# A graph network kernel on one core: the node update's second product one unit later in the turn

## The chip, the core and the metric

The kernel runs on one core of a Trainium2 chip. The metric is the time of one execution on the device in microseconds (us); smaller is better. The engines named below are TensorE (PE, with its weight loads as PEld), VectorE (DVE), ScalarE (ACT), GpSimd (POOL) and the queue of SyncE (SPq).

## What is computed

The input is a graph with 3,125 nodes of 256 features and 50,000 edges (sorted by target) with 16 features each. Two blocks follow each other, both of the form `x = x + block(relu(layernorm(x)))`. The first is a message network; the second is three graph convolutions over the same edges. Cut to what matters here:

```
h = relu(layernorm(x))
m = relu(concat(h[dst_side], h[src_side], e) @ mW1 + mb1)      # one row for each edge
agg = segment_sum(m @ mW2 + mb2)                                # one row for each node
u = relu(concat(h, agg) @ uW1 + ub1)                            # the node update's first product
x = x + h + (u @ uW2 + ub2)                                     # its second product, and the addition
h = relu(layernorm(x))
x = x + three graph convolutions(h, edges)
```

## The kernel before

Nodes are handled in 25 windows of 128 (`NW = 25`). Four stages run one after the other: `sort_and_embed` ranks the edges and makes the first layer's parts, `edge_mlp` runs the edge network and leaves for each window the sum of its hidden rows, `build_and_update` is the fused stage which the change touches, and `graph_layers` runs the three convolutions.

The fused stage does two things at once.

**Counting the adjacency matrix.** It is made in 175 blocks ("buckets") of 128 x 458 counts, by 568 build steps (`NS`). A step needs two one-hot matrices: `src_oh` (128 x 128, written by POOL on L1230 for three steps of four and by DVE on L1273 for the fourth) and `dst_oh` (128 x 458, always by DVE, L1275). PE multiplies them into one of four PSUM banks of `pC` (L1401). The slots for one-hots are eight deep. ACT reads a finished bank (L1485), prepares it for a later bucket (L1488) and stores the rows to `C_rows` (L1489). SPq lets PE into a bank only when ACT has prepared it (the semaphore `allowed`, L1348).

**The node update of each window.** PE turns the window's sums (`pS`, L1444), DVE copies them to `sT` (L1289); PE makes the message product into `pG` (L1411), DVE adds the bias to make `agg` (L1302); PE turns that (L1454), DVE copies it to `aggT` (L1308); PE makes the first update product into `pU` (`hidden`, L1423), DVE adds the known part (L1315) and takes the maximum with zero (L1317), which is `uT`; PE makes the second update product into `pX` (`update`, L1434, two halves of four matmul instructions in the trace), DVE adds it to the residual (L1295) and takes its statistics (L1297). Many of these tiles lie in one buffer, so the trace calls `sT`, `uT`, `agg`, `aggT` and the weights `sums`.

**The order is written by hand.** There are 27 turns of 9 units (0 to 8). Window i's messages are made in turn i, its first update product in turn i+1, its second in turn i+2. The 568 steps are spread evenly: `first_step(i, u)` is `(9 i + u) * 568 // 243`, so each unit holds two or three steps. PE issues in each unit first the unit's own piece of the update and then the unit's steps. DVE goes through the same units, but in each it first writes one-hots up to five steps beyond the unit's first step (`AHEAD = 5`), and then does the unit's own piece:

```
upto = min(NS, first_step(i, u) + AHEAD)
for s in range(made, upto):
    one_hots(s)
```

So the steps of PE's unit 0 are covered by the one-hots which DVE writes in units 7 and 8 of the turn before, and those of PE's unit 1 reach into the one-hots which DVE writes in its unit 0. DVE's pieces are: unit 0 `sT`, unit 2 the addition, unit 4 `agg`, unit 7 `aggT`, unit 8 `uT` (add and maximum). The copy `aggT` in unit 7 waits until PE has finished the first update product of its unit 8, since that product reads the old `aggT`. Each engine works through its instructions in this order.

Of the kernel before, what the change touches and what calls it, by code (L numbers as in the profile page):

```python
# [21 lines left out]
NW = -(-N // P)  # L22
# [1087 lines left out]
def build_and_update(nc, io, dr, keep):  # L1110


    with ExitStack() as stack:
# [82 lines left out]
        def first_step(i, u):  # L1196

            return min(NS, (i * UNITS + u) * NS // (TURNS * UNITS))

        def known_u(w):  # L1200

            if w < 12:
                return low[:, 2 * w:2 * w + 2, 0:D]
            if w < 14:
                return low[:, 2 * w - 12:2 * w - 10, D:2 * D]
            if w < 17:
                return low[:, 2 * w - 10:2 * w - 8, D:2 * D]
            return late_u[:, w - 17, :, :]
# [25 lines left out]
        def _(dve):  # L1234
# [34 lines left out]
            def one_hots(s):  # L1269
                if s >= SLOTS:  # L1270
                    dve.wait_ge(step_done, s - SLOTS + 2)
                if s % SHARE == 0:
                    v.tensor_scalar(src_oh[:, s % SLOTS, :], keep.iota16[:, :], src_s[:, s:s + 1], None,  # L1273
                                    ALU.is_equal).then_inc(src_own, 1)
                v.tensor_scalar(dst_oh[:, s % SLOTS, :], iota_cw[:, :], dst_s[:, s:s + 1], None, ALU.is_equal  # L1275
                                ).then_inc(dst_ready, 1)

            made = 0
            for i in range(TURNS):
                for u in range(UNITS):  # L1280
# [3 lines that stand above are left out]
                    made = max(made, upto)  # L1284
                    if u == 0 and i < NW:
                        dve.wait_ge(st_done, i + 1)
                        if i >= 1:
                            dve.wait_ge(agg_done, i)
                        v.tensor_copy(sT[:, :], pS[:, :]).then_inc(st_ready, 1)  # L1289
                    if u == 2 and 0 <= i - 2 < NW:  # L1290
                        w = i - 2
                        dve.wait_ge(x_done, w + 1)
                        dve.wait_ge(ub_added, w + 1)
                        r = keep.resid[:, w, :]
                        v.tensor_tensor(r, r, pX[:, 0:D], ALU.add).then_inc(x_ready, 1)  # L1295
                        dve.wait_ge(x_ready, w + 1)
                        v.bn_stats(stats[:, w, :], r).then_inc(stat_ready, 1)  # L1297
                    if u == 4 and i < NW:
                        dve.wait_ge(agg_done, i + 1)
                        if i >= 1:  # L1300
                            dve.wait_ge(at_done, i)
                        v.scalar_tensor_tensor(out=agg[:, :], in0=mb2[:, :], scalar=keep.deg_src[:, i:i + 1],  # L1302
                                               in1=pG[:, 0:D], op0=ALU.mult, op1=ALU.add).then_inc(agg_ready, 1)
                    if u == 7 and i < NW:
                        dve.wait_ge(at_done, i + 1)
                        if i >= 1:
                            dve.wait_ge(u_done, i)
                        v.tensor_copy(aggT[:, :], pG[:, D:2 * D]).then_inc(at_ready, 1)  # L1308
                    if u == 8 and 0 <= i - 1 < NW:
                        w = i - 1  # L1310
                        dve.wait_ge(u_done, w + 1)
                        if w >= 1:
                            dve.wait_ge(x_done, w)
                        dve.wait_ge(h_in[0 if w < HG else 1], 16 * (HG if w < HG else NW - HG))
                        link(v.tensor_tensor(uT.rearrange("p (b n) -> p b n", b=2),  # L1315
                                             pU[:, :].rearrange("p (b n) -> p b n", b=2), known_u(w), ALU.add))
                        v.tensor_scalar(uT, uT, 0.0, None, ALU.max).then_inc(u_ready, 1)  # L1317
# [33 lines left out]
        def _(pe):  # L1351
# [37 lines left out]
            def build_step(s):  # L1389
                if s % GRP == 0:  # L1390
                    _, got = nc.values_load_multi_w_load_instructions(
                        keep.step_bank[0:1, s:s + GRP], engines=[pe.engine], min_val=0, max_val=(BANKS - 1) * HID,
                        skip_runtime_bounds_check_because="the low bits of a bucket's number, times a bank's size")
                    at.update(enumerate(got))
                pe.wait_ge(allowed, s + 1)
                if s % SHARE:
                    pe.wait_ge(src_ready, s - s // SHARE)
                else:
                    pe.wait_ge(src_own, s // SHARE + 1)
                pe.wait_ge(dst_ready, s + 1)  # L1400
                mm(pC[:, bass.ds(at[s % GRP], CW)], src_oh[:, s % SLOTS, :], dst_oh[:, s % SLOTS, :], start=False,  # L1401
                   stop=False, skip_group_check=True).then_inc(step_done, 1)

            def message(i, half):
                if half == 0:
                    pe.wait_ge(st_ready, i + 1)
                    if i >= 1:
                        pe.wait_ge(agg_ready, i)
                        pe.wait_ge(at_ready, i)
                for k in range(2 * half, 2 * half + 2):  # L1410
                    last = mm(pG[:, 0:D], sT[:, k * P:(k + 1) * P], mw2[:, k, :], start=(k == 0), stop=(k == 3))  # L1411
                if half == 1:
                    last.then_inc(agg_done, 1)

            def hidden(w, m):
                if m == 0:
                    pe.wait_ge(at_ready, w + 1)
                    if w == 0:
                        pe.wait_ge(deg_copied, KP)
                    else:  # L1420
                        pe.wait_ge(u_ready, w)
                for k in range(2):
                    last = mm(pU[:, m * P:(m + 1) * P], uw1[:, 2 * (m // 2) + k, (m % 2) * P:(m % 2 + 1) * P],  # L1423
                              aggT[:, k * P:(k + 1) * P], start=(k == 0), stop=(k == 1))
                if m == 3:
                    last.then_inc(u_done, 1)

            def update(w, half):
                if half == 0:
                    pe.wait_ge(u_ready, w + 1)  # L1430
                    if w >= 1:
                        pe.wait_ge(x_ready, w)
                for k in range(2 * half, 2 * half + 2):
                    last = mm(pX[:, 0:D], uT[:, k * P:(k + 1) * P], uw2[:, k, :], start=(k == 0), stop=(k == 3))  # L1434
                if half == 1:
                    last.then_inc(x_done, 1)

            for i in range(TURNS):
                for u in range(UNITS):
                    if u == 0 and i < NW:  # L1440
                        if i >= 1:
                            pe.wait_ge(st_ready, i)
                        for k in range(4):
                            last = nc.tensor.transpose(pS[:, k * P:(k + 1) * P],  # L1444
                                                       keep.sums[:, 2 * i * HID + k * P:2 * i * HID + (k + 1) * P], keep.ident[:, :])
                        last.then_inc(st_done, 1)
                    if 1 <= u <= 2 and 0 <= i - 2 < NW:
                        update(i - 2, u - 1)
                    if 3 <= u <= 4 and i < NW:
                        message(i, u - 3)  # L1450
                    if u == 7 and i < NW:
                        pe.wait_ge(agg_ready, i + 1)
                        for k in range(2):
                            last = nc.tensor.transpose(pG[:, D + k * P:D + (k + 1) * P], agg[:, k * P:(k + 1) * P],  # L1454
                                                       keep.ident[:, :])
                        last.then_inc(at_done, 1)
                    if 5 <= u <= 8 and 0 <= i - 1 < NW:
                        hidden(i - 1, u - 5)
                    for s in range(first_step(i, u), first_step(i, u + 1)):
                        build_step(s)  # L1460
# [554 lines left out]
```

## Time and profile before

| what | value |
|---|---|
| time of the runs | 2148.41 us median of 3 (2143.78 to 2148.63) |
| time of the profiled execution | 2150.04 us |
| its span, first to last instruction | 2148.2 us |
| mean granted TensorE clock | 0.914 of full speed |
| busy share PE, DVE, POOL, ACT | 86%, 72%, 58%, 37% |
| the fused stage's build steps | 1274 to 1592 us of the span |

Busy shares are those of the whole span; the stages differ in what limits them, so the fused stage has to be read by itself. A wait in square brackets in the rows below is the idle time of an engine before an instruction, with the instruction that ended it. A row of several instructions gives the start of the first and the time from there to the end of the last. A wait of an engine that is not the bound costs nothing.

### The profile page before, as it was taken

Reading aid. Unit: us, or ns where it says so; the run is one execution under the profiler, and the core shown is the slowest. Engines: PE = TensorE matmul, PEld = TensorE weight load, DVE = VectorE, ACT = ScalarE, POOL = GpSimd, SP = SyncE. Lnnn points to the kernel's source line nnn. Section 1 sums busy time; section 2 is a strip of 40 time slices with the busy share of each in tenths; the row PEclk is TensorE's granted clock in tenths of the full one; section 3 lists DMA queues with packets and bytes.
Section 4 is the critical chain, followed back from the end, with each engine's and each line's share of the span. In section 5 each row is a group of like instructions: output and inputs, shape, how many; then the busy total and the mean of one; then the engine's idle time right before and its main releaser. Section 6 shows DMA issues by size and latency. Waiting matters only on the chain. (4 is left out here: it accounts for less than half of the span.)

```text
span 2148.2 us, 34105 instructions
## 1 busy us (share of the span) xinstructions
PE 1856.5 (86%) x8860; PEld 1252.2 (58%) x8860; DVE 1543.6 (72%) x4318; ACT 795.9 (37%) x1973; POOL 1241.1 (58%) x1461
## 2 busy tenths in 40 slices
PE   3677877775399999999999969998969999999997
PEld 2344454443155555555555536666647788788776
DVE  8877777776299988999988968988877345335332
ACT  0221222221155555555555536655662122113000
POOL 3777777777687777777777739998967000000000
PEclk7676777787699999999999979999999999999999
DMA  5111111111376666666666862212244234343232
GB/s 157 43 55 51 56 56 56 56 56 51 92 199 190 190 191 185 189 190 191 189 188 189 176 187 69 67 63 65 70 119 148 80 114 121 96 120 118 89 118 89
DMA packets 181702, 254.09 MB, mean 118 GB/s; under 512 B 29245, under 2 KB 144762, under 8 KB 181515
## 3 DMA queue, kind: packets, MB, share of 16 engines
q0 software_dynamic: 47888, 126.25, 21.6%
q1 hardware_dynamic: 101186, 99.11, 15.0%
q10 hardware_dynamic: 32440, 26.55, 3.8%
q8 instruction: 79, 1.29, 0.3%
q14 instruction: 109, 0.88, 0.1%
HBM read 202.35 MB, written 49.37 MB: 117 GB/s over the span
## 5 line engine op out<-in xcount | busy, mean ns | idle before, releaser
L971 POOL DMA_INDIRECT brow<-B_rows,rows x440 | 464.8, 1056 | 178.5 <-DVE pre L1074 109.8
L372 POOL DMA_INDIRECT src_list<-ring,ring_row x392 | 400.0, 1021 | 151.5 <-issue 117.6
L1865 PE MATMUL pO<-F,y 128*128 128x512 f32 x1728 | 436.4, 406 | 9.8 <-DVE y L1685 6.6
L1865 PEld LDWEIGHTS pO<-F,y 128*128 128x128 f32 x1728 | 326.8, 190 | 89.0 <-DVE y L1685 6.8
L1002 PE MATMUL pEdge<-A,turned 128*128 x880 | 333.2, 490 | 0.0
L1074 DVE TENSOR_TENSOR pre<-pEdge,brow 128x1024 f32<-128x1024 f32 x220 | 268.7, 1221 | 50.9 <-PE pEdge L1002 42.6
L1230 POOL TENSOR_SCALAR src_oh<-iota,src_s 128x128 bf16<-128x128 bf16 x426 | 281.1, 676 | 31.2 <-PE pC L1401 30.0
L1011 PE MATMUL pNode<-hid_whole,oh 128*128 128x512 f32 x440 | 227.7, 599 | 20.9 <-DVE sums L1092 20.9
L1681 DVE CAST F<-raw 128x512 fp32r<-128x512 uint16 x432 | 173.8, 439 | 66.8 <-PE pO L1865 61.6
L1036 ACT ACTIVATE turned<-pTurn 128x256 fp32r<-128x256 bf16 x220 | 84.8, 386 | 313.3 <-PE pTurn L990 313.3
L1275 DVE TENSOR_SCALAR dst_oh<-iota_cw,dst_s 128x458 bf16<-128x458 f16 x568 | 187.0, 376 | 0.0
L1401 PE MATMUL pC<-dst_oh,src_oh 128*128 128x458 bf16 x568 | 160.2, 365 | 29.7 <-SPq L1348 22.1
L1092 DVE SCALAR_TENSOR_TENSOR sums<-sums,going_on,pNode 128x512 f32 x220 | 163.2, 742 | 24.8 <-issue 23.7
L1002 PEld LDWEIGHTS pEdge<-A,turned 128*128 128x128 f32 x880 | 171.3, 195 | 11.8
L1013 PE MATMUL pNode<-hid_upper,oh 128*128 128x512 f32 x220 | 174.5, 793 | 0.0
L1000 PE MATMUL pEdge<-we_rows,turned_e 96*128 96x512 bf16 x440 | 170.3, 387 | 1.3 <-DVE pre L1074 0.9
L814 PE MATMUL pP<-U,upto 128*128 128x182 bf16 x385 | 48.3, 275 | 134.0 <-DVE posf L577 134.0
L1082 DVE SCALAR_TENSOR_TENSOR hid_lower<-pre,hid_upper 128x512 fp32r<-128x512 f32 x220 | 150.0, 682 | 0.0
L1485 ACT CAST c_rows<-pC 128x458 uint16<-128x458 f32 x175 | 94.7, 541 | 133.5 <-PE pC L1401 111.8
L1044 ACT ACTIVATE hid_whole<-pre 128x512 f32<-128x512 f32 x220 | 139.9, 636 | 6.4 <-DVE pre L1074 6.4
L1048 ACT ACTIVATE hid_upper<-pre 128x512 fp32r<-128x512 f32 x220 | 136.6, 621 | 0.0
L814 PEld LDWEIGHTS pP<-U,upto 128*128 128x128 bf16 x385 | 36.0, 110 | 144.0 <-DVE posf L577 132.2
(290 smaller groups left out, 3038.9 us busy)
## 6 DMA issues: line engine op xcount, KB each, us to landing
raw<-C_rows SPq DMA_DIRECT2D x72, 768.0 KB, 4.4
C_rows<-c_rows ACTq DMA_DIRECT2D x175, 114.5 KB, 1.7
rows<-src_list SPq DMA_DIRECT2D x110, 100.0 KB, 2.6
brow<-B_rows,rows POOLq DMA_INDIRECT x440, 3.7
U_parts<-part_u SPq DMA_DIRECT2D x25, 256.0 KB, 2.1
B_rows<-bst SPq DMA_DIRECT2D x25, 256.0 KB, 2.1
src_list<-ring,ring_row POOLq DMA_INDIRECT x392
sums<-U_parts SPq DMA_DIRECT2D x17, 256.0 KB, 5.8
```

The costliest lines, as they stand in the source:

```text
L372: nc.gpsimd.indirect_dma_start(dr.src_list[:, :, :].rearrange("p t w -> (p t) w"), bass.IndirectOffsetOnAxis(ap=ring_row[:, k % RING, t:t ...
L971: nc.gpsimd.indirect_dma_start(brow[:, t % BR, :], None, dr.B, bass.IndirectOffsetOnAxis(ap=rows_i[:, m % LCS, j, 1:2], axis=0)).then_inc( ...
L1000: mm(to, turned_e[:, p % 2, n * P:(n + 1) * P], keep.we[:, :], start=True, stop=False)
L1002: last = mm(to, turned[:, p % 2, n * P:(n + 1) * P], keep.A[:, 2 * HID + k * HID:][:, bass.ds(at[p], HID)], start=False, stop=(k == 1))
L1011: mm(pN[p % 2][:, :], oh[:, q % OHQ, j, :].bitcast(F32), whole[:, p % WHOLE, :], start=True, stop=False)
L1013: mm(pN[p % 2][:, :], oh[:, q % OHQ, j + 1, :], upper[:, p % SPLIT, :], start=False, stop=False)
L1074: v.tensor_tensor(pre[:, p % 2, :], pE[p % 2][:, :], brow[:, at_row:at_row + 2, :].rearrange("p t n -> p (t n)"), ALU.add).then_inc(pre_re ...
L1092: v.scalar_tensor_tensor(out=keep.sums[:, bass.ds(at[p], HID)], in0=keep.sums[:, bass.ds(at[max(p - 1, 0)], HID)], scalar=keep.going_on[:, ...
L1230: nc.gpsimd.tensor_scalar(src_oh[:, s % SLOTS, :], keep.iota16[:, :], src_s[:, s:s + 1], None, ALU.is_equal).then_inc(src_ready, 1)
L1275: v.tensor_scalar(dst_oh[:, s % SLOTS, :], iota_cw[:, :], dst_s[:, s:s + 1], None, ALU.is_equal).then_inc(dst_ready, 1)
L1681: v.tensor_copy(F[:, n % FS, :], raw[:, m % RAWS, n % RAWW, :]).then_inc(f_ready, 1)
L1865: last = mm(pO[m % 2][half][:, :], y[:, win, part, half * P:(half + 1) * P], F[:, n % FS, :], start=(win == 0 and part == 0), stop=False)
```

## The change

The second update product of window i-2 moves from PE's units 1 and 2 to its units 2 and 3 of turn i. The addition of its result, with the statistics, moves from DVE's unit 2 to its unit 4, where it stands ahead of `agg`. PE's unit 3 then holds the second half of the product and the first half of the message product; unit 1 holds nothing but its steps. No instruction is added or removed, and no transfer moves.

```
                        v.tensor_copy(sT[:, :], pS[:, :]).then_inc(st_ready, 1)
-                    if u == 2 and 0 <= i - 2 < NW:
+                    if u == 4 and 0 <= i - 2 < NW:
                         w = i - 2
                         dve.wait_ge(x_done, w + 1)
...
                         last.then_inc(st_done, 1)
-                    if 1 <= u <= 2 and 0 <= i - 2 < NW:
-                        update(i - 2, u - 1)
+                    if 2 <= u <= 3 and 0 <= i - 2 < NW:
+                        update(i - 2, u - 2)
                     if 3 <= u <= 4 and i < NW:
                         message(i, u - 3)
```

## Rows read from the trace of the kernel before

**Rows 1.** The page's head and its first part: busy time of each engine.

```profile
span 2148.2 us, 34105 instructions
PE 1856.5 (86%) x8860; PEld 1252.2 (58%) x8860; DVE 1543.6 (72%) x4318; ACT 795.9 (37%) x1973; POOL 1241.1 (58%) x1461
```

**Rows 2.** The chain that ended last, its first pieces after the fused stage.

```profile
1595.54 6.51 DMA raw<-C_rows
```

**Rows 3.** Busy time by stretch: the stage, turns 11 and 12, two clock stretches.

```profile
core 0: us, PE busy (x) PEld busy (x) DVE busy (x) ACT busy (x) POOL busy (x), PEclk, DMA share, GB/s
1298.00:1592.00 294.00, 263.73 (x1428) 186.50 (x1427) 263.25 (x850) 175.61 (x324) 273.71 (x413) 0.99 0.21 67
1400.62:1412.47 11.85, 10.57 (x60) 7.77 (x59) 10.26 (x33) 6.96 (x13) 11.45 (x17) 1.00 0.19 63
1412.47:1426.31 13.84, 12.26 (x61) 8.62 (x58) 11.30 (x34) 7.17 (x14) 11.50 (x18) 0.88 0.16 53
1412.31:1415.72 3.41, 1.83 (x11) 0.91 (x9) 3.11 (x8) 1.89 (x4) 3.41 (x6) 1.00 0.22 71
1415.72:1419.13 3.41, 3.41 (x9) 2.27 (x10) 2.61 (x10) 1.09 (x2) 2.13 (x4) 0.50 0.00 0
```

**Rows 4.** Waits from 1298 to 1592 us: total, times, longest.

```profile
ACT c_rows L1485 <- PE pC L1401: 93.3, 125, 3.5
DVE sums L1308 <- PE pU L1423: 21.2, 23, 2.1
POOL src_oh L1230 <- PE pC L1401: 18.1, 34, 2.4
PE pX L1434 <- DVE sums L1317: 13.6, 23, 1.0
PE pC L1401 <- SPq L1348: 9.7, 14, 1.5
PE pC L1401 <- DVE dst_oh L1275: 5.3, 15, 0.7
```

**Rows 5.** Waits of PE in the stage's last stretch, 1560 to 1592 us.

```profile
PE pC L1401 <- SPq L1348: 5.6, 6, 1.5
```

**Rows 6.** PE and DVE in order of time, start of turn 11.

```profile
1401.07 0.33 DVE L1275 TENSOR_SCALAR dst_oh<-iota_cw,dst_s 128x458 bf16<-128x458 f16 x1
1401.64 0.36 PE L1401 MATMUL pC<-dst_oh,src_oh 128*128 128x458 bf16 x1 [0.19 <-DVE dst_oh L1275]
1402.51 0.36 PE L1401 MATMUL pC<-dst_oh,src_oh 128*128 128x458 bf16 x1 [0.51 <-DVE dst_oh L1275]
1402.97 0.43 DVE L1317 TENSOR_SCALAR sums<-sums 128x512 f32<-128x512 f32 x1
1403.31 0.72 DVE L1275 TENSOR_SCALAR dst_oh<-iota_cw,dst_s 128x458 bf16<-128x458 f16 x2
1403.45 1.13 PE L1434 MATMUL pX<-sums 128*128 128x256 f32 x4 [0.58 <-DVE sums L1317]
1404.42 0.75 PE L1401 MATMUL pC<-dst_oh,src_oh 128*128 128x458 bf16 x3
```

**Rows 7.** The same at the start of turn 4.

```profile
1322.16 0.72 DVE L1275 TENSOR_SCALAR dst_oh<-iota_cw,dst_s 128x458 bf16<-128x458 f16 x2
1322.30 1.13 PE L1434 MATMUL pX<-sums 128*128 128x256 f32 x4 [0.51 <-DVE sums L1317]
1323.27 0.55 PE L1401 MATMUL pC<-dst_oh,src_oh 128*128 128x458 bf16 x2
```

**Rows 8.** The same at the start of turn 21.

```profile
1524.52 1.13 PE L1434 MATMUL pX<-sums 128*128 128x256 f32 x4 [0.51 <-DVE sums L1317]
1524.66 0.75 DVE L1275 TENSOR_SCALAR dst_oh<-iota_cw,dst_s 128x458 bf16<-128x458 f16 x2
1525.48 0.55 PE L1401 MATMUL pC<-dst_oh,src_oh 128*128 128x458 bf16 x2
```

**Rows 9.** The moved instructions on DVE, turn 11, in order of time.

```profile
1406.35 0.40 DVE L1295 TENSOR_TENSOR resid<-resid,pX 128x256 f32<-128x256 f32 x1
1406.78 0.43 DVE L1297 BATCH_NORM_STATS2 stats<-resid 128x6 f32<-128x256 f32 x1
```

More of the change, by code:

```diff
@@ L1289, in _ @@
                         v.tensor_copy(sT[:, :], pS[:, :]).then_inc(st_ready, 1)
-                    if u == 2 and 0 <= i - 2 < NW:
+                    if u == 4 and 0 <= i - 2 < NW:
                         w = i - 2
@@ L1446, in _ @@
                         last.then_inc(st_done, 1)
-                    if 1 <= u <= 2 and 0 <= i - 2 < NW:
-                        update(i - 2, u - 1)
+                    if 2 <= u <= 3 and 0 <= i - 2 < NW:
+                        update(i - 2, u - 2)
                     if 3 <= u <= 4 and i < NW:
```

## Prediction

> **What bounds the kernel now.** I read the page's busy times first [rows 1]. They say little of this change, since every engine's share is an average over four stages. The chain that ended last begins only at 1595 us, with the load of the counts that the fused stage stored [rows 2]. The last stage therefore starts when the fused stage ends, and whatever the fused stage gains or loses reaches the end in full. So the whole question lies between 1274 and 1592 us.
>
> There the busy times by stretch come next [rows 3]: from 1298 to 1592 us PE is busy for 263.7 of 294 us, DVE for 263.3, POOL for 273.7. Three engines have nearly the same load, so busy time does not name the bound and the waits must [rows 4]. ACT waits for PE for 93 us, DVE for 21 us (the copy `aggT`), POOL for 18 us. PE waits for others for less than 30 us: 13.6 us for `uT`, 5.3 us for `dst_oh`, 9.7 us for a bank. The loop that sets the pace is one between PE and DVE. At the end of a turn PE finishes the first update product, which frees DVE's `aggT` copy; DVE then writes one-hots, makes `uT`, and writes more one-hots, while PE runs out of work; from there on PE is dense until the next end of a turn. The order of time at the start of turn 11 shows it [rows 6]: PE stands for 0.19, 0.51 and 0.58 us, and for nothing in the rest of that row of work.
>
> **The change, part by part.** Nothing is added, so the cost is one of order.
>
> *What is taken away.* PE no longer stands before `update` for `uT`: by the time it comes to unit 2, `uT` is long done. That is up to 13.6 us over 23 waits [rows 4], a mean of 0.59 us.
>
> *What comes in its place.* Unit 1 now holds only its steps. By the kernel's order DVE's unit 8 has written one-hots for 2.67 steps past the start of the turn, and unit 0's PE steps use 2.33 of them. The steps of unit 1, which reach to 4.67, need those of DVE's unit 0, and DVE writes these after `uT`. Before, PE covered that time with half an update product, which needed only `uT`. Now it has nothing to cover it with, and waits for the last `dst_oh` of unit 1, which is later than `uT`.
>
> For turn 11 [rows 6]: a one-hot that ended at 1401.07 + 0.33 = 1401.40 let its step start at 1401.64, so the way from DVE to PE is 0.24 us. Two steps in a row take 0.55 where one takes 0.36 [rows 7], so each further step is 0.19 to 0.20 us. The last one-hot that unit 1 needs ends at 1403.31 + 0.72 = 1404.03. Its step starts at 1404.27, and the update product at 1404.47, where it started at 1403.45: 1.02 us later. The three steps that used to follow it are by then done, and are worth 3 x 0.195 = 0.59 us. Net: PE stands 0.43 us later in its work than before.
>
> For turn 4 [rows 7]: last one-hot 1322.16 + 0.72 = 1322.88, product at 1323.32 in place of 1322.30, less two steps (0.39): 0.63 us. For turn 21 [rows 8]: last one-hot 1524.66 + 0.75 = 1525.41, product at 1525.85 in place of 1524.52, less 0.39: 0.94 us. Nine turns have three steps in unit 1 as turn 11 has, the rest two. The mean of the three is 0.67 us. PE is dense from there to the end of the turn, DVE's `aggT` copy waits for PE and so comes later by the same amount, and the next turn begins that much later. Nothing in the loop gives it back. Over the 24 turns from 2 to 25: 24 x 0.67 = 16 us. By the lowest and the highest of the three it is 10 and 23 us.
>
> *The addition on DVE.* L1295 and L1297 take 0.40 and 0.43 us [rows 9], some 0.86 us with the gap between them, and move from unit 2 to unit 4. Behind them on DVE now stands `agg` and then the one-hots of unit 5. PE needs `agg` only in unit 7. The one-hots of units 3 and 4 come 0.86 us sooner, but PE did not stand for them. What could be gained is DVE's wait for `pX`, and what could be lost is an `agg` that is late; with three units of some 1.2 us between, I take nothing for both. At the most the addition lies bare in each turn, 24 x 0.86 = 21 us, or gives as much, but DVE's 21 us of waits for PE [rows 4] speak against both.
>
> *What swallows part of it.* Where a bank is late, PE waits for ACT through SPq, and a PE that comes later waits less. There are 9.7 us of such waits [rows 4], 5.6 us of them from 1560 us on [rows 5], where the last turns follow ACT. I take the last two turns' delay as hidden there (0.94 + 0.67 = 1.6 us) and 1 us elsewhere. The bound from below is 0, from above 9.7 us.
>
> *The clock.* In turn 12 PE stood still for 1.58 us of the 3.41 us before 1415.72 and then ran at a granted clock of 0.50 (1.2 GHz) until 1419.13; the turn took 13.84 us in place of turn 11's 11.85 [rows 3]. A fall costs 2.0 us. My gaps at the start of turn 11 come to 0.19 + 0.51 us as now, and then, in place of 0.58 us, one of about 0.9 before the second step of unit 1, so about 1.6 us in place of 1.3. More gaps can only make falls likelier, though the clock stayed at 1.00 through turn 11. I take half a fall more than now, 1 us; the bounds are one fewer (-2 us) and five more (+10 us).
>
> The Trainium skill's page "TensorE: Matmul & The Clock Gate" (section "A second HAM failure mode: psum-queue depth-cycling") says that short idles between groups of matmuls can be enough to make the clock go to and fro. This trace agrees in one turn: 0.50 after gaps none of which was long. By that rule alone each turn might fall, and the sum would be some 48 us more; the same gaps of 1.3 us in turn 11 left the clock at 1.00 [rows 3], so the sum above doesn't follow it.
>
> *Sum.* 16.1 - 1.6 - 1.0 + 1.0 = 14.5 us. The profiled execution took 2150.04 us, of which 1.84 lie outside its span of 2148.2 and stay. It gives 2164.5. That execution was 1.6 us above the median of the runs shown, 2148.41, from which I would get 2162.9. I forecast 2164 us.
>
> **The rivals.** A measurement of this kernel can tell about 0.3%, 6.4 us, from no change.
>
> *The clock falls in many turns.* For it: PE stands longer at the start of each turn, and turn 12 fell after standing for 1.58 us [rows 3]. Against: the gaps grow by a third only, and those of turn 11 left the clock alone. Five falls more are 14.5 + 9 = 24 us, a fall in each of ten turns 35 us: 2173 to 2184 us.
>
> *The wait is absorbed, and no change shows.* The banks are the mechanism: if PE's later arrival saves all of its 9.7 us of waits for SPq, and the least of the three turns holds (10 us), nothing is left; with one clock fall fewer the time is 2148 to 2154. Against it: ACT waits 93 us for PE, so in most of the stage it is ACT that is early.
>
> *Faster: the wait for `uT` goes and nothing replaces it.* This would be so if the one-hots for unit 1 were ready when PE comes to it, that is, if the last of them ended before 1402.5 in turn 11 rather than at 1404.03. It decides at that point: each turn then wins its 0.59 us. With 13.6 us of waits gone, and perhaps the two falls of the clock (4 us), it gives 2136 down to 2132 us. For it: the wait on `uT` is real and the longest item of PE's list, and DVE has 0.86 us less to do before its unit 3. Against it: that work stands behind the one-hots in question, not ahead of them, and `uT` itself is ahead of them.
>
> **How the numbers follow.** My forecast (a later one-hot takes the wait's place, few falls more) has 0.66, its own range 2157 to 2171. More falls of the clock have 0.14, all slower. Absorbed has 0.11, mostly within 0.3%. Faster has 0.09, of which 0.07 goes beyond 0.3%. The forecast's lower end lends 0.03 to no change. Slower: 0.80, same: 0.13, faster: 0.07. The range is 2152 to 2174: it leaves out the faster case and the upper part of the falls.
>
> **What would show it.** Right: in the stage PE's wait for L1317 is gone, and its wait for `dst_oh` (L1275) grows from 5.3 to some 30 us; the start of turn 4 shows one gap of about 1 us inside unit 1's steps; turns are 12.3 us in place of 11.8; DVE's wait before L1308 grows from 21 to some 35 us; POOL and ACT wait more; the last stage has the same length. The addition's own wait (L1295) is near nothing. Wrong: turns no longer than before, which means that one-hots were ready or that another engine had been the pace; new waits of PE before L1454, which means that `agg` is late; or a granted clock in the stage well under 0.99, which is the rival with the falls.

## The result and the profile after

The changed kernel took 2166.07 us (median of 5 runs, 2164.43 to 2169.25), the kernel before 2147.29 us in the same comparison. The ratio is 1.0089 with a 95% interval of 1.0076 to 1.0103: slower by 19 us, with 16 to 22 us inside the interval. The forecast was 2164 us, slower, from a loss of 14.5 us.

The head of the page answers to [rows 1]: the work is the same, the span is 15 us longer.

```profile
span 2163.2 us, 34105 instructions
PE 1858.8 (86%) x8860; PEld 1252.1 (58%) x8860; DVE 1540.1 (71%) x4318; ACT 795.2 (37%) x1973; POOL 1237.0 (57%) x1461
```

The start of turn 4 after the change, PE, DVE and POOL in order of time; it answers to [rows 7]:

```profile
1323.60 5.66 POOL L1230 TENSOR_SCALAR src_oh<-iota,src_s 128x128 bf16<-128x128 bf16 x9
1325.33 0.42 DVE L1308 COPY sums<-pG 128x256 f32<-128x256 f32 x1 [0.62 <-PE pU L1423]
1326.42 0.72 PE L1401 MATMUL pC<-dst_oh,src_oh 128*128 128x458 bf16 x2 [0.17 <-SPq L1348]
1327.16 0.43 DVE L1317 TENSOR_SCALAR sums<-sums 128x512 f32<-128x512 f32 x1
1327.51 0.72 DVE L1275 TENSOR_SCALAR dst_oh<-iota_cw,dst_s 128x458 bf16<-128x458 f16 x2
1328.19 0.64 PE L1401 MATMUL pC<-dst_oh,src_oh 128*128 128x458 bf16 x2 [1.06 <-POOL src_oh L1230]
1328.67 1.03 PE L1434 MATMUL pX<-sums 128*128 128x256 f32 x4
```

PE has finished unit 0's two steps at 1327.14 and stands for 1.06 us until the first step of unit 1. The row names POOL as what ended the wait. It was not: POOL wrote nine one-hots in a row without idle, and the one of this step had ended 2.8 us earlier. DVE's two one-hots start at 1327.51, behind the maximum of `uT`, and their rows end at 1327.95 and 1328.23; PE's steps start 0.24 us behind each, at 1328.19 and 1328.47. The product follows at 1328.67. From the end of the first update product (0.10 us ahead of `aggT`, so 1325.23) it starts 3.44 us on. In the kernel before that product of turn 3 ended at 1319.82, and the second one started 1322.30 - 1319.82 = 2.48 us on [rows 7]. The gap has moved from ahead of the product (0.51 us) to ahead of the steps (1.06 us).

The waits, in the same order as [rows 4] but from 1298 to 1608 us, the longer stage:

```profile
POOL src_oh L1230 <- PE pC L1401: 33.2, 52, 1.8
DVE sums L1308 <- PE pU L1423: 23.7, 24, 1.5
PE pC L1401 <- DVE dst_oh L1275: 19.7, 31, 1.6
DVE sums L1302 <- PE pG L1411: 14.4, 21, 1.2
PE pC L1401 <- SPq L1348: 12.7, 19, 2.0
PE pC L1401 <- POOL src_oh L1230: 8.0, 13, 1.1
DVE resid L1295 <- PE pX L1434: 0.9, 1, 0.9
```

PE's wait for L1317 (13.6 us) is gone from the list. Its waits on L1401 put down to DVE and POOL were 5.3 us and almost nothing; they are now 19.7 + 8.0 us. The names are not to be trusted here, for SPq no more than for POOL: in turn 7 a wait of 0.97 us is put down to SPq, and it too ended 0.24 us behind the step's `dst_oh`. The distance to the step's own `dst_oh` is the better sign. In turns 2 to 25 the changed kernel's steps have 58 waits of at least 0.15 us, and 43 of them end 0.24 us behind the end of that one-hot. Waits with this sign (0.24 us, in a few cases up to 0.30) come to 5.8 us in the kernel before and to 27.4 us in the changed one. Of these, 22.4 us stand before steps of unit 1, where the kernel before has none.

**Where the 15 us between the two profiled spans lie.** I cut both traces at the first build step, at the end of the first update product in turn 1 and in turn 25 (24 turns, 2 to 25, lie between), and at the first matmul of the last stage. The rows give busy time by stretch, for the 24 turns of the kernel before and then for the piece behind them up to the last stage:

```profile
core 0: us, PE busy (x) PEld busy (x) DVE busy (x) ACT busy (x) POOL busy (x), PEclk, DMA share, GB/s
1296.68:1578.76 282.08, 257.20 (x1403) 183.57 (x1401) 254.18 (x800) 170.46 (x314) 265.61 (x401) 0.99 0.21 67
1578.76:1595.82 17.06, 7.85 (x32) 3.66 (x33) 11.02 (x58) 6.73 (x13) 9.42 (x15) 1.00 0.19 62
```

and for the changed one:

```profile
1300.24:1592.71 292.47, 255.81 (x1404) 181.91 (x1401) 253.49 (x800) 169.74 (x313) 262.92 (x400) 1.00 0.20 65
1592.71:1611.91 19.20, 10.44 (x33) 4.90 (x33) 11.35 (x59) 7.35 (x15) 10.22 (x16) 0.77 0.17 56
```

| piece | before | after | difference |
|---|---|---|---|
| up to the first build step | 1274.4 | 1278.7 | +4.3 |
| from there to the end of turn 1 | 22.3 | 21.5 | -0.8 |
| 24 turns | 282.1 | 292.5 | +10.4 |
| turn 26 and the rest of the stage | 17.1 | 19.2 | +2.1 |
| last stage | 552.4 | 551.3 | -1.1 |

The first piece runs the same instructions in both and is not the change's. The 24 turns of the kernel before hold two falls of the clock, turns of 13.84 and 13.99 us; the other 22 have a mean of 11.56 us. The changed kernel has no fall in these turns, and their mean is 12.19 us. So a turn at full clock has grown by 0.63 us, 24 x 0.63 = 15.1 us, and with the 2.1 us of the end this is 17 us of the 19 measured.

### The profile page after: what moved, and what is told of

Read it like the earlier page. It is cut to its first block and busy times, and to the rows that moved or that the text cites. A ratio compares the mean times of both kernels' runs of the same rounds, so it can differ in the third digit from the quotient of the medians.

```text
span 2163.2 us, 34105 instructions
## 1 busy us (share of the span) xinstructions
PE 1858.8 (86%) x8860; PEld 1252.1 (58%) x8860; DVE 1540.1 (71%) x4318; ACT 795.2 (37%) x1973; POOL 1237.0 (57%) x1461
## 5 line engine op out<-in xcount | busy, mean ns | idle before, releaser
L1401 PE MATMUL pC<-dst_oh,src_oh 128*128 128x458 bf16 x568 | 164.4, 365 | 55.3 <-SPq L1348 25.6
L1401 PEld LDWEIGHTS pC<-dst_oh,src_oh 128*128 128x128 bf16 x568 | 55.9, 98 | 116.7 <-issue 99.0
## 6 DMA issues: line engine op xcount, KB each, us to landing
U_parts<-part_u SPq DMA_DIRECT2D x25, 256.0 KB, 2.1
B_rows<-bst SPq DMA_DIRECT2D x25, 256.0 KB, 2.1
sums<-U_parts SPq DMA_DIRECT2D x17, 256.0 KB, 5.6
```

## The experiments

Each was timed in five rounds against the kernel before. The first four (the addition alone, the product alone, and AHEAD = 7 on both kernels) ran on a chip on which the kernel before takes 2284.63 us (the later ones: 2144.60 and 2146.03), so ratios are compared and not times. The 137 us more lie ahead of the 24 turns, which begin there at 1434 us of the span and not at 1297, so the same loss makes a slightly smaller ratio there: 19 us are 0.88% of 2147 and 0.83% of 2285 us. The length of a turn can be compared directly: it is the mean over those of the 24 turns in which the granted clock stayed at 1.00. That length and the number of falls come from one profiled execution of each kernel.

| kernel | ratio, 95% interval | turn at full clock, us | turns with a fall |
|---|---|---|---|
| before | 1 | 11.56 | 2 |
| the change | 1.0089 (1.0076 to 1.0103) | 12.19 | 0 |
| addition alone | 0.9988 (0.9977 to 1.0000) | 11.62 | 0 |
| product, addition one unit | 1.0090 (1.0073 to 1.0107) | 12.28 | 4 |
| product in units 3 and 4 | 1.0241 (1.0222 to 1.0261) | 13.24 | 11 |
| before, AHEAD = 7 | 0.9990 (0.9979 to 1.0001) | 11.45 | 1 |
| change, AHEAD = 6 | 1.0042 (1.0027 to 1.0056) | 11.85 | 0 |
| change, AHEAD = 7 | 0.9982 (0.9971 to 0.9992) | 11.30 | 0 |
| change, uT behind unit 0's one-hots | 1.0067 (1.0050 to 1.0083) | 12.09 | 1 |
| before, uT first | 1.0043 (1.0027 to 1.0059) | 11.83 | 1 |
| before, uT first, AHEAD = 7 | 0.9955 (0.9939 to 0.9971) | 11.25 | 0 |
| change, uT first, AHEAD = 7 | 0.9996 (0.9987 to 1.0006) | 11.45 | 1 |
| uT first, AHEAD = 7, one in three | 0.9946 (0.9933 to 0.9960) | 11.05 | 0 |
| uT first, AHEAD = 7, one in five | 0.9984 (0.9975 to 0.9993) | 11.46 | 0 |

### Which half of the change costs: the addition alone

Edits to the kernel before:

```
-                    if u == 2 and 0 <= i - 2 < NW:
+                    if u == 4 and 0 <= i - 2 < NW:
```

> The kernel before, with only the addition (L1295) and its statistics moved from DVE's unit 2 to its unit 4; the product stays in PE's units 1 and 2. Theory A (what costs is that PE has nothing to do in unit 1 until DVE's one-hots behind uT are written): no change, 2147 us, within 4 us of the kernel before. Theory B (what costs is the addition standing ahead of agg on DVE, 0.86 us in each turn): most of the 19 us, 2160 to 2166 us, and DVE's waits before agg (L1302) as long as after the change.

Measured: ratio 0.9988, turns of 11.62 us. The addition's place costs nothing. DVE's waits before `agg` did not grow: in the 24 turns they are 0.7 us, where the kernel before has 1.6.

### The product alone

Edits to the kernel before:

```
-                    if u == 2 and 0 <= i - 2 < NW:
+                    if u == 3 and 0 <= i - 2 < NW:
...
-                    if 1 <= u <= 2 and 0 <= i - 2 < NW:
-                        update(i - 2, u - 1)
+                    if 2 <= u <= 3 and 0 <= i - 2 < NW:
+                        update(i - 2, u - 2)
```

> The kernel before, with the product moved to PE's units 2 and 3 and the addition moved by one unit only, to DVE's unit 3, the first at which it can follow the product. Theory A: the loss of the whole change, 2162 to 2168 us. Theory B: within 4 us of the kernel before. If it is slower than the change itself, the addition's later place had bought something, since in unit 3 DVE would stand for the product.

Measured: 1.0090, the whole loss. The waits of its 24 turns show the one difference from the change: DVE stands for the product in unit 3.

```profile
PE pC L1401 <- DVE dst_oh L1275: 19.2, 31, 1.5
DVE sums L1302 <- PE pG L1411: 11.8, 20, 0.7
DVE resid L1295 <- PE pX L1434: 8.6, 9, 2.0
```

Those 8.6 us make the turns 0.09 us longer at most (12.28 against 12.19), and the ratios are the same. The later place of the addition bought DVE free time, and no time of the kernel that these runs can tell.

### The one-hots for unit 1 written ahead of uT

On the changed kernel:

```
-        AHEAD = 5
+        AHEAD = 7
```

> The change, with AHEAD = 7 in place of 5: DVE's unit 8 then writes all one-hots that PE's unit 1 needs, and writes them ahead of uT. The number of one-hots in each unit stays as it was. Theory A: PE's gap of about 1.05 us in unit 1 goes, PE comes to the product about 2.1 us after the end of the first product, when uT is 0.1 to 0.4 us from ready; each turn loses 0.6 to 1.0 us of idle against the change: 2140 to 2150 us, at or under the kernel before. Rival (PE stands in unit 1 for POOL or for a bank, as the trace names them for some of these waits): no change, 2166 us. Rival B: no change either.

Measured: 0.9982, turns of 11.30 us in place of 12.19. The loss is gone, and more. The waits in its 24 turns:

```profile
PE pC L1401 <- SPq L1348: 9.7, 12, 2.2
PE pX L1434 <- DVE sums L1317: 7.4, 16, 0.9
PE pC L1401 <- DVE dst_oh L1275: 1.8, 5, 0.5
PE pC L1401 <- POOL src_oh L1230: 0.6, 2, 0.4
```

In the 24 turns the wait for DVE's one-hots fell from 19.4 to 1.8 us, and with it the one that the trace had put down to POOL, from 7.6 to 0.6 us, although POOL's work and order had not changed. That settles whose wait it was: by the sign of 0.24 us the waits behind a step's own `dst_oh` are 27.4 us under the change and 1.3 us here. What is left is a wait of 7.4 us for `uT`, shorter than the 13.6 us of the kernel before. In whole time 0.9982 of 2147 is 2143 us, inside the 2140 to 2150 that I had given.

### The same on the kernel before

```
-        AHEAD = 5
+        AHEAD = 7
```

> The kernel before, with AHEAD = 7. Theory A: PE's gap at the start of a turn ends with uT, wherever the one-hots are, so that earlier one-hots only lengthen the wait for uT by what they save on dst_oh: within 4 us of the kernel before. Rival (each wait counts by itself): PE's 5.3 us of waits for dst_oh go, 2141 to 2143 us.

Measured: 0.9990, or 2 us less, within the 4 us. The interval (0.9979 to 1.0001) reaches to 4.5 us and so just touches the rival's 4 to 6 us; the time alone doesn't decide between the two, the waits do. Waits in its 24 turns:

```profile
PE pX L1434 <- DVE sums L1317: 25.8, 23, 2.0
PE pC L1401 <- DVE dst_oh L1275: 0.2, 1, 0.2
```

The wait for `dst_oh` went from 5.3 to 0.2 us, and that for `uT` rose from 13.6 to 25.8 us. With the product in unit 1 the gap ends with `uT`, and what PE gets ahead of that is worth little (0.11 us a turn). The sum of the two rose by 7 us although the time did not. I read that as a matter of the record: a step that waits shows its whole 0.36 us as busy, one that follows another adds 0.19 us [rows 6], so a gap broken up by steps counts as less idle than the same gap in one piece.

### Half of the cover

On the changed kernel:

```
-        AHEAD = 5
+        AHEAD = 6
```

> The change with AHEAD = 6. Theory A: one one-hot fewer of those which unit 1 needs stands behind uT, so the last of them comes 0.3 us sooner in each of 24 turns: 7 to 8 us of the loss come back, turns of 11.85 to 11.95 us in place of 12.19, 1.004 to 1.006 of the kernel before. Rival (only a full cover helps, or the loss has another source): 1.009.

Measured: 1.0042, turns of 11.85 us: 0.34 us less than under the change, the length of about one one-hot. The three settings 5, 6 and 7 give 12.19, 11.85 and 11.30 us, so each one-hot that stands ahead of `uT` in place of behind it is paid back by about its own length or more.

### One unit further

Edits to the kernel before:

```
-                    if u == 2 and 0 <= i - 2 < NW:
+                    if u == 5 and 0 <= i - 2 < NW:
...
-                    if 1 <= u <= 2 and 0 <= i - 2 < NW:
-                        update(i - 2, u - 1)
+                    if 3 <= u <= 4 and 0 <= i - 2 < NW:
+                        update(i - 2, u - 3)
```

> One unit further still: the product in PE's units 3 and 4, the addition in DVE's unit 5. Theory A: units 1 and 2 now both follow DVE's one-hots, and the half product that the change still had in unit 2 (some 0.9 us) no longer covers those behind sT. Each of 24 turns loses 0.86 to 0.97 us more than under the change: 21 to 23 us more, 1.018 to 1.020 of the kernel before. Rival (a fixed price for taking the product out of unit 1, whatever comes after): 1.009, as the change.

Measured: 1.0241, more than expected. PE at the start of a turn:

```profile
1337.03 0.60 PE L1444 MATMUL pS<-ident,sums 128*128 128x128 f32 x4
1337.47 0.55 PE L1401 MATMUL pC<-dst_oh,src_oh 128*128 128x458 bf16 x2
1338.93 0.36 PE L1401 MATMUL pC<-dst_oh,src_oh 128*128 128x458 bf16 x1 [0.91 <-DVE dst_oh L1275]
1339.79 0.64 PE L1401 MATMUL pC<-dst_oh,src_oh 128*128 128x458 bf16 x2 [0.49 <-DVE dst_oh L1275]
1340.92 0.72 PE L1401 MATMUL pC<-dst_oh,src_oh 128*128 128x458 bf16 x2 [0.49 <-DVE dst_oh L1275]
1341.48 1.04 PE L1434 MATMUL pX<-sums 128*128 128x256 f32 x4
```

Units 1 and 2 both follow DVE now: three gaps of 0.91, 0.49 and 0.49 us. By the sign of 0.24 us these waits are 24.3 us in unit 1 and 12.3 us in unit 2, where the change has 22.4 and 0.3 us. A turn at full clock is 13.24 us, 1.05 us above the change, a little over the 0.86 to 0.97 expected. The rest is the clock. The row of its 24 turns:

```profile
1293.43:1625.08 331.65, 280.08 (x1404) 193.91 (x1401) 253.76 (x800) 170.30 (x314) 266.27 (x401) 0.94 0.17 57
```

Eleven of the 24 turns hold a stretch at 0.50. At 13.24 us all 24 would take 317.8 us, so the turns with a fall cost 13.9 us more than that, 1.3 us each. The rival of many falls did not come true for the change itself, but one unit further it did.

### uT behind unit 0's one-hots

The change, with this block moved to the next turn's unit 0, ahead of `sT`:

```
-                    if u == 8 and 0 <= i - 1 < NW:
-                        w = i - 1
+                    if u == 0 and 0 <= i - 2 < NW:
+                        w = i - 2
```

> The change, with uT (L1315 and L1317) written on DVE behind the one-hots of unit 0 of the next turn instead of ahead of them. Theory A: the one-hots of PE's unit 1 come 1.1 us sooner and PE's gap there goes; the product in unit 2 then waits for a uT that ends when the last of these one-hots ended under the change, and starts 0.05 us behind it in place of 0.44 us. Each turn wins about 0.4 us of the change's loss: 1.004 to 1.006 of the kernel before, with the wait on uT (L1317) back and the wait on L1275 in unit 1 gone. Rival (the loss has another source than the order on DVE): 1.009.

Measured: 1.0067, turns of 12.09 us. The direction is as expected and so is the exchange of the waits: PE's waits of unit 1 for one-hots are 0.7 us by the sign of 0.24 us, and the wait for `uT` (now L1293) is back with 10.9 us. The gain is a quarter of what I gave (0.10 us a turn, not 0.4). A turn's start in this kernel, turn 6, PE and DVE:

```profile
1349.88 0.86 DVE L1275 TENSOR_SCALAR dst_oh<-iota_cw,dst_s 128x458 bf16<-128x458 f16 x3
1350.91 0.58 PE L1401 MATMUL pC<-dst_oh,src_oh 128*128 128x458 bf16 x2 [0.51 <-DVE dst_oh L1275]
1351.37 0.43 DVE L1293 TENSOR_SCALAR sums<-sums 128x512 f32<-128x512 f32 x1
1351.85 1.13 PE L1434 MATMUL pX<-sums 128*128 128x256 f32 x4 [0.36 <-DVE sums L1293]
```

In this turn the product starts 3.20 us after the first product's end (1348.65). The wait of 0.51 us in it is not DVE's, whatever its name: this step's one-hots had ended 0.7 us or more before it started. Over the 24 turns the product starts 3.38 us after the first product's end, against 3.72 us under the change (and 2.54 in the kernel before). So 0.34 us of the expected 0.4 was won at that point. But the product's second half ends 6.22 us after the first product, against 6.25 under the change: by then the gain is gone. That would fit DVE's queue, in which all that unit 0 holds, `uT` included, is the same work in either order, so that the one-hots of PE's unit 2 come no sooner; I did not test it.

### uT first, with and without more one-hots ahead

In both, `uT` is written right behind `aggT`; in the second AHEAD is 7 as well.

```
-                    if u == 8 and 0 <= i - 1 < NW:
+                    if u == 7 and 0 <= i - 1 < NW:
```

> The same with AHEAD = 5, as before. Theory A: uT is early, but the one-hots of PE's unit 0 now stand behind it, and PE comes to the product about 2.9 us after the end of the first product in place of 2.5: 24 x 0.4 = 10 us slower, 1.003 to 1.006 of the kernel before. Rival (the wait for uT is the one that counts, so that an earlier uT is a gain by itself): 0.995.

> The kernel before with its product in units 1 and 2, AHEAD = 7, and uT written on DVE right behind aggT, ahead of unit 8's one-hots. Theory A: uT is ready 1.7 us after the end of the first product in place of 2.4, and PE comes to it at about 1.75 us: nearly no idle is left at the start of a turn. PE's work alone would give turns of 10.9 us (262 us for 24), POOL's 11.3 us (271 us), so POOL sets them: 0.995 to 0.997 of the kernel before, about as the change with AHEAD = 7. If it reaches 265 us or less for the 24 turns, POOL was not the next bound.

Measured: 1.0043 with AHEAD = 5, and 0.9955 with 7. Both are inside what was expected. An early `uT` alone is a loss: the one-hots of unit 0 now stand behind it. The waits of the 24 turns, first with 5:

```profile
PE pC L1401 <- DVE dst_oh L1275: 17.7, 17, 1.7
PE pC L1401 <- POOL src_oh L1230: 10.9, 9, 1.8
PE pC L1401 <- SPq L1348: 8.1, 7, 1.8
```

The names mislead again: by the sign of 0.24 us, 32.1 us are waits of unit 0's steps for their own `dst_oh` (5.4 us in the kernel before). The waits with AHEAD = 7:

```profile
PE pC L1401 <- SPq L1348: 6.0, 11, 1.8
PE pX L1434 <- DVE sums L1317: 5.0, 13, 0.8
PE pC L1401 <- DVE dst_oh L1275: 2.2, 4, 1.1
```

### The product's place once both covers are there

The change with `uT` first and AHEAD = 7 (the two edits above).

> The change with both mends: AHEAD = 7 and uT right behind aggT. Theory A with POOL as the next bound: no idle of PE is left for the product's place to matter, so it is within 0.15% of the same kernel with the product in units 1 and 2: 0.994 to 0.997 of the kernel before, turns of 11.2 to 11.3 us. Rival (a product in unit 2 is worse by itself, whatever DVE has ready): 0.4% or more slower than with the product in units 1 and 2.

Measured: 0.9996 against 0.9955 for the same kernel with the product in units 1 and 2. My expectation was wrong and the rival as I had worded it came true, though in the main not for a reason of its own. I had not followed DVE's queue: with `uT` first, all of unit 8's one-hots stand behind it, and with the product gone from unit 1 PE comes to them bare. Its order of time shows it; the step that waits starts 0.24 us behind its `dst_oh` here too, although the row names POOL:

```profile
1352.30 0.55 PE L1401 MATMUL pC<-dst_oh,src_oh 128*128 128x458 bf16 x2
1352.60 0.43 DVE L1317 TENSOR_SCALAR sums<-sums 128x512 f32<-128x512 f32 x1
1352.94 1.06 DVE L1275 TENSOR_SCALAR dst_oh<-iota_cw,dst_s 128x458 bf16<-128x458 f16 x3
1353.63 0.64 PE L1401 MATMUL pC<-dst_oh,src_oh 128*128 128x458 bf16 x2 [0.78 <-POOL src_oh L1230]
```

`uT` is ready at 1353.03 with PE free at 1352.85; a product there would have cost 0.2 us of idle where the steps cost 0.78. The turns at full clock account for 24 x 0.20 = 4.8 us of the 8.8 us between the two ratios. One fall of the clock (2.4 us) and a longer end of the stage (19.6 us against 17.3) make up the rest, as far as single profiles can tell. That end is longer in each kernel with the product in units 2 and 3, whatever one-hots it has ready (see *What swallows part of it* below), so some 2 us of the rival are its own.

### What bounds the turn next

On the kernel with `uT` first and AHEAD = 7, the share of the source one-hots that DVE writes (and in a second kernel SHARE = 5):

```
-        SHARE = 4
+        SHARE = 3
```

> The kernel with uT first and AHEAD = 7, and one source one-hot in three written by DVE in place of one in four: POOL loses 47 of its 426 (31 us), DVE gains 47 (about 12 us). If POOL sets the 11.25 us turns: 0.991 to 0.994 of the kernel before. If DVE is as near its limit as POOL (its waits at the end of a turn sum up to 12 us): no gain or slower than with one in four, 0.996 or above.

> The same with one source one-hot in five written by DVE: POOL gains 28 (19 us), DVE loses 28 (7 us). If POOL sets the turns: most of the 19 us, 1.000 to 1.005 of the kernel before. If DVE does: 0.993 to 0.995.

Measured: 0.9946 with one in three, 0.9984 with one in five, against 0.9955 with one in four. Turns of 11.05, 11.46 and 11.25 us. The rows of the 24 turns, one in three and then one in five:

```profile
1294.80:1560.11 265.31, 247.66 (x1403) 181.04 (x1401) 256.00 (x839) 170.42 (x314) 246.37 (x357) 1.00 0.22 71
```

```profile
1293.63:1568.63 275.00, 253.96 (x1404) 179.71 (x1401) 254.00 (x772) 170.25 (x314) 274.72 (x425) 1.00 0.21 69
```

With one in five POOL is busy for 274.7 of 275.0 us, and with one in four for 268.3 of 269.9: it sets the turn. With one in three DVE is busy for 256.0 and PE for 247.7 of 265.3 us, and no engine is full. Neither kernel came out as forecast: 0.9946 lies between the two ranges given for one in three (0.991 to 0.994 if POOL sets the turns, 0.996 or above if DVE does), and 0.9984 between the two for one in five. The second miss can be read from the profiles: POOL wrote 25 one-hots more in the 24 turns, but was busy for only 6.4 us more, since one of them took 661 ns on the mean in place of 687 (703 with one in three). POOL's one-hot is not of fixed length: it was longer in the kernels in which DVE wrote more of them. The order of the three fits POOL as the bound at four and five; the step from four to three (0.9955 to 0.9946) lies inside both intervals and is shown by the turns only. The kernel with one in three is the fastest of all: 2134.05 against 2146.03 us.

## Why the prediction was right

The mechanism was right, and so was the size of its main term. That the total came within some 2 us is in part luck. The forecast was of 14.5 us of loss where 18.8 were measured, and 14.5 lies below the interval of 16 to 22 us. It was added to a profiled execution of 2150.04 us, 2.8 us above the 2147.29 of the comparison, which hid most of the difference.

*The bound and the way to the end.* Right. The last stage's length changed by 1.1 us only (552.4 and 551.3 us), and what the fused stage lost was lost by the kernel.

*What is taken away and what takes its place.* Right, and shown from several sides: the wait for `uT` went, the wait for one-hots behind `uT` came. The product alone brings the whole loss; one-hots ahead of `uT` take it away in two steps; the place of the addition has no part in it. PE's waits by name came to 27.7 us for DVE and POOL together, where I had some 30 for `dst_oh`.

*The sum of the turns.* 0.67 us by three turns, 16.1 us in all; measured 0.63 and 15.1 us. The three turns themselves scatter more than their mean shows: turns 4, 11 and 21 grew by 0.65, 0.21 and 0.67 us, where I had 0.63, 0.43 and 0.94, so part of the nearness of 16.1 to 15.1 is chance. The sum also left out turn 26, in which the last product is made. The 1.02 us by which I had the product start later in turn 4 was 3.44 - 2.48 = 0.96 us.

*The addition on DVE.* Nothing, as taken. Where DVE's waits would show up I had wrong: I expected them before `aggT` (21 to 35 us), and they came before `agg` (L1302, from 1.6 to 14.4 us in the 24 turns) while those before `aggT` stayed (22.1 and 23.7 us). My reading, not tested, is that DVE comes to unit 4 while PE is late, and that from there on both are as far apart as before.

*What swallows part of it.* Wrong in its sign. I had 2.6 us hidden behind ACT in the last turns and elsewhere. Turn 25 was shorter (9.83 us, where it was 10.35), but that isn't the change's: it took 9.74 us with the addition alone, whose product had not moved. Turn 26 and the end of the stage took 2.1 us more. Rows of PE from there, the kernel before and then the changed one:

```profile
1586.41 1.92 PE L1401 MATMUL pC<-dst_oh,src_oh 128*128 128x458 bf16 x8 [1.51 <-SPq L1348]
```

```profile
1598.77 1.91 PE L1434 MATMUL pX<-sums 128*128 128x256 f32 x4
1603.17 2.32 PE L1401 MATMUL pC<-dst_oh,src_oh 128*128 128x458 bf16 x10
```

Before, both halves of the product were done at 1584.71 and PE then waited for banks all the same (1.51 us, and 1.34 us once more); a product that ends sooner would have gained nothing there. After the change it comes behind waits for banks, and ten steps follow it without a wait. PE's waits for banks fell in this piece from 5.1 to 4.0 us only. The piece is longer in every kernel with the product in units 2 and 3 (18.7 to 19.7 us in six) than in those with it in units 1 and 2 (17.1 to 17.6 us in seven). With AHEAD = 7 on the changed kernel it is 19.2 us, although its turns have lost nothing, so the one-hots behind `uT` are not what costs here.

The clock has at most a part in it. Up to the last build step the changed kernel holds 6.8 us at 0.50 in this piece, and the kernel before none. But four of the seven (the addition alone and three of those with `uT` first) have 3.4 us of it there and take 17.2 to 17.6 us, and the product alone has 3.4 us as well and takes 18.7. How much of the 2.1 us is the clock's stays open.

*The clock.* The price of 2.0 us was about right: turns with a fall took 13.95, 13.95 and 13.84 us in three kernels whose other turns took 11.45, 12.09 and 11.83, which is 1.9 to 2.5 us. The number was not: I took half a fall more than the two, on the ground that more gaps can only make falls likelier; the changed kernel's profile has more gaps and no fall in the 24 turns. (The growth of the gaps from 1.3 to 1.6 us, which I called a third, is a quarter.) The product alone, with nearly the same gaps, has four. So neither the gain of 4.7 us that two fewer give this profile nor the loss of a fall more is the change's; the ratio of five runs holds a mean over them. Between the two profiles this term was 5.7 us too high (+1.0 against -4.7) and the one before it 4.7 us too low (-2.6 against +2.1), so they nearly cancelled.

The rule of the Trainium skill's page "TensorE: Matmul & The Clock Gate" (section "A second HAM failure mode: psum-queue depth-cycling"), that short idles between matmul groups can be enough, is borne out by the product in units 3 and 4: gaps of 0.91, 0.49 and 0.49 us, and eleven turns of 24 with a fall. The changed kernel, with gaps of 1.06 us, had none in its 24 turns.

## What to carry to other kernels

When an engine waits for X, moving the consumer of X later helps only if the work that moves up in its place needs nothing that stands behind X in the producer's queue; otherwise the wait changes its name and grows by what the consumer used to cover. So write down, for each piece of the waiting engine, which entry of the producer's queue it needs last, and give the gap to the piece which needs the earliest. Change the supply first (here AHEAD and the place of `uT` together, 0.9955, where each alone gave 0.9990 and 1.0043), and look for the bound that comes next. Look at the ends of the pipeline too: in the last turn the product had been done beside waits for banks, and with the product moved the end of the stage took some 2 us more, with more one-hots ahead as without.

## What was not expected of the hardware

- The releaser that a row names can be the wrong one where an instruction waits for several. A wait of 1.06 us was put down to POOL, whose one-hot had been there for 2.8 us, and such waits fell from 7.6 to 0.6 us in the 24 turns when only DVE's order changed. The distance from the end of the step's `dst_oh` to PE's start was the surer sign: it was 0.24 us in 43 of the 58 waits of the changed kernel's steps in its 24 turns, some of them put down to POOL or SPq.
- Falls of the granted clock differ widely between kernels with nearly the same gaps: none in 24 turns with the change, four with the product alone, at turns of 12.19 and 12.28 us. Each such profile is one execution; a turn at full clock told the kernels apart better than the span did.
- The stages ahead of the fused one run the same instructions in all the kernels, yet their length differed by up to 8.8 us between profiles on the chips where the kernel takes some 2146 us (first build step at 1269.9 to 1278.7 us). A difference of a few us between two single profiles has to be placed in its stage before it is explained.
